# A DLRM interaction tower: embedding rows staged in DRAM by chunks, near and far loaded in one transfer each

## What is computed

```
x1 = relu(einsum('bhd,bmd,ohm->bod', e, e, W1) + b1)              # o = 128
x2 = relu(einsum('bhd,bmd,ohm->bod', x1[:, :64], e, W2) + b2)     # o = 128
z  = sum over d of concat(x1[:, 64:], x2)                         # 192 numbers per sample
```

## Time and profile before

| | |
|---|---|
| median of 3 runs | 2021.38 us (2020.23 to 2021.54) |
| profiled execution, its own time | 2020.18 us |
| its span in the profile | 2018.4 us |
| TensorE busy (matmul records) | 99% |
| VectorE, ScalarE, GpSimd busy | 95%, 83%, 68% |
| DMA engines, bytes over the span | 482.57 MB, 239 GB/s |

### The profile page before, as it was taken

One profiled execution on the slowest core, in us unless ns is written; L12 is line 12 of the kernel. 1 busy time (PEld: TensorE's weight loads), 2 busy tenths in 40 slices (PEclk: granted clock), 3 DMA queues, 4 the chain that ended last, 5 costly groups with the idle time before them and its releaser, 6 DMA issues.

```text
span 2018.4 us, 24272 instructions
## 1 busy us (share of the span) xinstructions
PE 1991.0 (99%) x7030; PEld 1322.2 (66%) x7030; DVE 1920.1 (95%) x672; ACT 1671.3 (83%) x4953; POOL 1370.3 (68%) x647
## 2 busy tenths in 40 slices
PE   5999999999999999999999999999999999999999
PEld 3666666666666666666666666666666666666664
DVE  6999999999999999999999999999999999999992
ACT  3888888888888888888888888888888888888884
POOL 5767867777677767768667668677767768677520
PEclk9999999999999999999999999999999999999999
DMA  7999999989989999999999999999999999998960
GB/s 214 261 262 245 263 239 243 259 240 243 258 240 243 254 244 243 252 247 242 250 250 241 249 252 240 248 251 241 249 251 239 247 253 240 247 254 240 244 174 11
DMA packets 272119, 482.57 MB, mean 239 GB/s; under 512 B 37473, under 2 KB 70753, under 8 KB 271858
## 3 DMA queue, kind: packets, MB, share of 16 engines
q1 hardware_dynamic: 244786, 404.58, 66.7%
q0 software_dynamic: 26624, 75.52, 21.7%
q10 hardware_dynamic: 576, 0.92, 0.1%
HBM read 313.10 MB, written 16.78 MB: 163 GB/s over the span
## 4 chain that ended last, share of the span: by engine, by line
PE 97%; DMA 1%; POOL 1%; issue 0%; SPq 0%; ACT 0%; DVE 0%; POOLq 0%; ACTq 0%
PE acc L618 21%; PE acc L630 19%; PE acc L637 19%; PE acc L631 19%; PE acc L642 16%; PE acc L621 1%; POOL gathered L272 0%; DMA plo_dma<-pnear 0%; PE x1p L721 0%; PE acc L721 0%; DMA gathered<-in_tables,idx_all 0%; DMA x1rep<-x 0%; DMA near<-emb_rows 0%; PE acc L728 0%; PE x1p L600 0%
## 5 line engine op out<-in xcount | busy, mean ns | idle before, releaser
L305 POOL TENSOR_TENSOR prod<-near,h 128x2048 f32<-128x2048 f32 x126 | 581.5, 4615 | 442.3 <-DMA near<-emb_rows 287.7
L630 PE MATMUL acc<-phi,w2lo 128*128 128x512 f32 x1664 | 704.4, 423 | 0.9 <-ACT phi L838 0.9
L631 PE MATMUL acc<-phi,w2hi 128*128 128x512 f32 x1664 | 651.8, 392 | 0.0
L534 DVE TENSOR_TENSOR pnear<-near,x1p 128x2048 f32<-128x2048 f32 x254 | 568.8, 2282 | 3.2 <-DMA plo_dma<-pnear 3.1
L527 DVE TENSOR_TENSOR pfar<-far,x1p 128x4096 f32<-128x4096 f32 x128 | 565.3, 4417 | 0.0
L272 POOL DMA_INDIRECT gathered<-in_tables,idx_all x256 | 495.5, 1935 | 71.5 <-issue 68.2
L845 ACT CAST phi<-pfar 128x2560 fp32r<-128x2560 f32 x128 | 300.2, 2345 | 216.5 <-PE acc L631 183.6
L618 PE MATMUL acc<-prod,w1T 128*128 128x512 f32 x1024 | 460.2, 592 | 1.5 <-DVE prod L507 1.5
L538 DVE TENSOR_TENSOR plo<-pnear,phi 128x3072 fp32r<-128x3072 f32 x128 | 433.5, 3386 | 0.0
L538 DVE TENSOR_TENSOR plo<-pfar,phi 128x2560 fp32r<-128x2560 f32 x128 | 361.7, 2826 | 41.1 <-ACT phi L845 40.7
L630 PEld LDWEIGHTS acc<-phi,w2lo 128*128 128x128 f32 x1664 | 313.1, 188 | 96.5 <-issue 30.4
(11 more groups left out here) (77 smaller groups left out, 1258.6 us busy)
## 6 DMA issues: line engine op xcount, KB each, us to landing
far<-emb_rows SPq DMA_DIRECT2D x512, 256.0 KB, 4.1
near<-emb_rows SPq DMA_DIRECT2D x510, 256.0 KB
plo_dma<-pnear POOLq DMA_DIRECT2D x128, 512.0 KB
x1rep<-x SPq DMA_DIRECT2D x255, 256.0 KB
h<-emb_rows SPq DMA_DIRECT2D x128, 256.0 KB
emb_rows<-gathered SPq DMA_DIRECT2D x127, 128.0 KB
rem_parts<-rem_hi SPq DMA_DIRECT2D x128, 64.0 KB
gathered<-in_tables,idx_all POOLq DMA_INDIRECT x256
```

The source lines that it names most:

```text
L305: nc.gpsimd.tensor_tensor(prod1[:, :, :], near[(u + 2) % 3][:, :, :], h0[odd][:, :].unsqueeze(1).to_broadcast([P, K1, N]), ALU.mult).then_ ...
L534: return nc.vector.tensor_tensor(pnear[:, a, :, :], near[u % 3][:, :, :], factor.unsqueeze(1).to_broadcast([P, K1, N]), ALU.mult)
L630: nc.tensor.matmul(acc2[s][:, :], w2lo[:, t, :], phi[:, t, :], start=(t == T_DMA), stop=False)
L631: mm = nc.tensor.matmul(acc2[s][:, :], w2hi[:, t, :], phi[:, t, :], start=False, stop=(t == T_SPLIT - 1))
```

## The change

- The DRAM array becomes one block of 64 rows x 512 numbers per chunk (128 KB, rows 2 KB apart).
- Tile k now pairs row i with row i + 4q + k. The four rows that a partition needs for `near` then lie side by side, and so do those for `far`: each becomes one transfer of 1 MB with 128 runs of 8 KB (it was four of 256 KB with runs of 2 KB). The weights are laid out to match (`diagonals`).
- The partitions of `gathered` are now (half of the pair, feature, part of the half). `store_copy` still writes 128 runs of 1 KB, in two blocks of 64 runs.
- The remainder works on 96 partitions in place of 64 (32 of them unused), `move_upper` moves 96, and six transfers place it in place of three.
- The table offsets are loaded by ScalarE in two halves (SP in one before), and the conversion of the indices is two copies in place of one.
- In the start, SP issues `h0` of chunk 0 and ScalarE all of `near` of chunk 0 (two tiles each before).

The diff, cut to its core; the other places follow from it (waits on the new counts, `c * N` in place of which stands `c`):

```diff
--- before.py
+++ after.py
@@ -20,10 +20,12 @@
-ROW = B * D + 1024
 SH = P // F
+CHUNK = 2 * F * N
 HALF = F // 2
 REM = 2 * HALF
+REM_ROWS = P - REM
@@ -58,7 +60,7 @@
-        emb = nc.dram_tensor("emb_rows", [2 * F, ROW], fp32, kind="Internal")
+        emb = nc.dram_tensor("emb_rows", [CHUNKS, CHUNK], fp32, kind="Internal")
@@ -82,10 +84,11 @@
-        rem_b = sb("rem_b", [HALF * GS, PAIR_GATHERS, D])
+        rem_b = sb("rem_b", [REM_ROWS, PAIR_GATHERS, D])
...
@@ -191,14 +194,15 @@
+        PLACES = 16 * 3 * 2
-        LOADS = 16 * (1 + K1)
+        LOADS = 16 * 2
...
-            return bass.AP(base.tensor, base.offset, [list(base.ap[0]), [SH, K1], [65, F], [1, SH]])
+            return bass.AP(base.tensor, base.offset, [list(base.ap[0]), [1, K1], [65, F], [SH, SH]])
@@ -236,20 +240,20 @@
         def store_copy(eng, f0, pair, s):
-            dst = bass.AP(emb, f0 * ROW + pair * (2 * N), [[ROW, F], [PAIR_GATHERS * D, GS], [1, PAIR_GATHERS * D]])
+            dst = bass.AP(emb, pair * (2 * CHUNK) + f0 * N, [[CHUNK, 2], [PAIR_GATHERS * D, P // 2], [1, PAIR_GATHERS * D]])
             eng.dma_start(dst, gathered[s][:, :, :]).then_inc(emb_stored, 16)
+        def load_h0(eng, c, s2, s3):
+            eng.dma_start(h0[s2][:, :], bass.AP(emb, c * CHUNK, [[N, F], [0, SH], [1, N]])).then_inc(near_in[s3], 16)
+
+        def load_near_tiles(eng, c, s3):
+            src = bass.AP(emb, c * CHUNK, [[N, F], [SH * N, SH], [1, K1 * N]])
+            eng.dma_start(near[s3][:, :, :].rearrange("p k n -> p (k n)"), src).then_inc(near_in[s3], 16)
...
-            sp.dma_start(table_row[:, :], a["table_rows"]).then_inc(ids_in, 16)
...
+            def load_far(c, s):
+                src = bass.AP(emb, c * CHUNK + HALF * N, [[N, F], [SH * N, SH], [1, K2 * N]])
+                sp.dma_start(far[s][:, :, :].rearrange("p k n -> p (k n)"), src).then_inc(far_in[s], 16)
             def move_upper(pair, s):
...
-                sp.dma_start(rem_b[:, :, :], gathered[s][HALF * GS:F * GS, :, :]).then_inc(rem_b_in, 16)
+                sp.dma_start(rem_b[:, :, :], gathered[s][REM:P, :, :]).then_inc(rem_b_in, 16)
...
                 for b, part in enumerate((rem_hi, rem_hi, rem_lo)):
-                    home = rem_parts[pair % 2][b * REM:(b + 1) * REM, :].rearrange("r (w n) -> r w n", w=2)
-                    sp.dma_start(home.bitcast(fp32), part[:, :].bitcast(fp32)).then_inc(rem_in, 16)
+                    for u in range(2):
+                        home = rem_parts[pair % 2][b * REM + u * HALF:b * REM + (u + 1) * HALF, :].rearrange("r (w n) -> r w n", w=2)
+                        sp.dma_start(home.bitcast(fp32), part[u * 2 * REM:u * 2 * REM + REM, :].bitcast(fp32)).then_inc(rem_in, 16)
@@ -376,8 +379,7 @@
             load_h0(sp, 0, 0, 0)
-            load_near_tiles(sp, 0, 0, range(0, K1 // 2))
-            load_near(sp, N, 1, 1)
+            load_near(sp, 1, 1, 1)
@@ -444,9 +446,12 @@
-            dve.wait_ge(ids_in, 32)
-            nc.vector.tensor_copy(ids_f[:, :, :].rearrange("r g (f q) -> r g f q", q=GS),
-                                  ids_n[:, :, :, :].rearrange("r q g f -> r g f q")).then_inc(ids_float, 1)
+            dve.wait_ge(ids_in, 48)
+            for w in range(2):
+                last = nc.vector.tensor_copy(
+                    ids_f[:, :, w * P // 2:(w + 1) * P // 2].rearrange("r g (f q) -> r g f q", f=F),
+                    ids_n[:, w * GS // 2:(w + 1) * GS // 2, :, :].rearrange("r q g f -> r g f q"))
+            last.then_inc(ids_float, 1)
@@ -768,9 +773,13 @@
+            for w in range(2):
+                nc.scalar.dma_start(table_row[w * P // 2:(w + 1) * P // 2, :],
+                                    a["table_rows"].rearrange("(f w q) one -> w f q one", w=2, q=GS // 2)[w]).then_inc(ids_in, 16)
             act.wait_ge(ident_ready, 1)
@@ -785,7 +794,7 @@
-            load_near_tiles(nc.scalar, 0, 0, range(K1 // 2, K1))
+            load_near_tiles(nc.scalar, 0, 0)
```

More of the change, by code:

```diff
@@ L82, in build_dlrm @@
         far = [sb(f"far_{s}", [P, K2, N]) for s in range(2)]
-        rem_b = sb("rem_b", [HALF * GS, PAIR_GATHERS, D])
-        rem_prod = sb("rem_prod", [HALF * GS, PAIR_GATHERS * D])
-        rem_hi = sb("rem_hi", [HALF * GS, PAIR_GATHERS * D], fp32r)
-        rem_lo = sb("rem_lo", [HALF * GS, PAIR_GATHERS * D], fp32r)
+        rem_b = sb("rem_b", [REM_ROWS, PAIR_GATHERS, D])
+        rem_prod = sb("rem_prod", [REM_ROWS, PAIR_GATHERS * D])
+        rem_hi = sb("rem_hi", [REM_ROWS, PAIR_GATHERS * D], fp32r)
+        rem_lo = sb("rem_lo", [REM_ROWS, PAIR_GATHERS * D], fp32r)
         rem_parts = [sb(f"rem_parts_{s}", [3 * REM, N], fp32r) for s in range(2)]
@@ L238, in store_copy, with load_near @@
         def store_copy(eng, f0, pair, s):
-            dst = bass.AP(emb, f0 * ROW + pair * (2 * N), [[ROW, F], [PAIR_GATHERS * D, GS], [1, PAIR_GATHERS * D]])
+            dst = bass.AP(emb, pair * (2 * CHUNK) + f0 * N, [[CHUNK, 2], [PAIR_GATHERS * D, P // 2], [1, PAIR_GATHERS * D]])
             eng.dma_start(dst, gathered[s][:, :, :]).then_inc(emb_stored, 16)
[L242 to L252, removed]
+        def load_h0(eng, c, s2, s3):
[3 more added lines that the diff above has]
+            eng.dma_start(near[s3][:, :, :].rearrange("p k n -> p (k n)"), src).then_inc(near_in[s3], 16)
+        def load_near(eng, c, s2, s3):
+            load_h0(eng, c, s2, s3)
+            load_near_tiles(eng, c, s3)
         def replicate_x1(eng, halves):
@@ L280, in remainder_products @@
                     pool.wait_ge(rem_lo_ready, pair)
-                nc.gpsimd.tensor_tensor(rem_prod[:, :], gathered[s][0:HALF * GS, :, :].rearrange("p g d -> p (g d)"),
+                nc.gpsimd.tensor_tensor(rem_prod[:, :], gathered[s][0:REM_ROWS, :, :].rearrange("p g d -> p (g d)"),
                                         rem_b[:, :, :].rearrange("p g d -> p (g d)"), ALU.mult).then_inc(rem_prod_ready, 1)
@@ L392, in _ @@
             sp.wait_ge(p1_ready, 1)
-            load_near(sp, 2 * N, 0, 2)
+            load_near(sp, 2, 0, 2)
             sp.wait_ge(w2_wide, 1)
             sp.wait_ge(w2_second, 1)
-            load_far(N, 1)
+            load_far(1, 1)
             def load_top():
@@ L428, in step @@
                         sp.wait_ge(emb_stored, STORES * (pair + 3))
-                    load_near(sp, (c + 3) * N, 1 - odd, u % 3)
+                    load_near(sp, c + 3, 1 - odd, u % 3)
                 if not odd and within(at, 5):
@@ L434, in step @@
                     sp.wait_ge(pfar_ready, c + 1)
-                    load_far((c + 2) * N, odd)
+                    load_far(c + 2, odd)
                 if at == 3:
@@ L473, in _ @@
             for u in range(2):
-                hi0, lo1, hi2 = (w1rem[u][:, b * REM + u:(b + 1) * REM:2] for b in range(3))
+                hi0, lo1, hi2 = (w1rem[u][:, b * REM + u * HALF:b * REM + (u + 1) * HALF] for b in range(3))
                 nc.vector.tensor_copy(hi0, w16hi[:, :].bitcast(fp32))
@@ L554, in step @@
                     dve.wait_ge(x1p_ready, 1)
-                dve.wait_ge(far_in[odd], 16 * K2 * (turn * (U // 2)) + 16 * K2 * (u // 2 + 1))
+                dve.wait_ge(far_in[odd], 16 * (turn * (U // 2)) + 16 * (u // 2 + 1))
                 if begun(at):
@@ L649, in _ @@
             tiles1(0, range(K1 // 2, K1))
-            pe.wait_ge(rem_in, 48)
+            pe.wait_ge(rem_in, PLACES)
             remainder1(0, 0)
@@ L676, in step @@
                     pe.wait_ge(p1_ready, c + 3)
-                    pe.wait_ge(rem_in, 48 * (pair + 2))
+                    pe.wait_ge(rem_in, PLACES * (pair + 2))
                     pe.wait_ge(z1_ready, c + 1)
@@ L770, in remainder_hi @@
                 if pair:
-                    act.wait_ge(rem_in, 48 * pair)
+                    act.wait_ge(rem_in, PLACES * pair)
                 nc.scalar.copy(rem_hi[:, :], rem_prod[:, :]).then_inc(rem_hi_ready, 1)
+            for w in range(2):
+                nc.scalar.dma_start(table_row[w * P // 2:(w + 1) * P // 2, :],
+                                    a["table_rows"].rearrange("(f w q) one -> w f q one", w=2, q=GS // 2)[w]).then_inc(ids_in, 16)
             act.wait_ge(ident_ready, 1)
```

## The result

The changed kernel takes 2124.45 us (median of 4 runs, 2118.89 to 2137.88) against 2020.81 us of before (4 runs). The ratio is 1.0524, 95% interval 1.049 to 1.0559: slower, +103.6 us. The profiled execution took 2121.54 us, its span is 2119.6.

The account below looks back on a forecast made before the run. TensorE bound the kernel before; DMA engines 0 and 1 would bind after, at 31.7 us a pair against 30.37. The profiled 2020.2 + 80 steady + 5 start = 2105, 2106 against the median; range 2019 to 2170 us.

Parts of the forecast that it names:

- The bound of before: In the steady part before the change, TensorE alone sets the time, 30.37 us per pair of chunks.
- Two engines for a store: The new store has outermost dimension 2, so two DMA engines carry it, 64 runs each.
- The store of pair 0: In the start, both stores put 128 runs on each of two engines; near of chunk 0 lands about 6 us later.
- A run of 1 KB: Price of one store or remainder packet on a DMA engine: 54 ns.
- Engines 0 and 1 become the bound: Stores add 6.0 us on these DMA engines; they need 31.7 us a pair against 30.37, so +80 us in all.
- The sign I had named for few engines: q1's mean share of the 16 DMA engines falls, with GB/s down, while time goes up.
- `near` and `far`: -1.2 us on every engine: Per pair, 128 runs of 2 KB (11.5 us) become 32 of 8 KB (10.3 us) on each DMA engine.
- Three issues more, +1.8 us of SP: Six transfers place the remainder in place of three, adding 1.8 us of SP's issue time per pair.
- bounds nothing: Six fewer SP issues per chunk save 7.2 us of SP a pair, said not to limit the time.
- The third rival: SP's in-order queue stalls behind store runs, delaying the replication of x1: 2170 us and up, chance 0.13.
- The start: Stores of pair 0 lie on the path before the steady part: +5 us, bounds 0 and +10.
- the offsets on ScalarE: Table offsets' loads in the start, counted among items within 0.5 us either way and left out.

Follow-up runs that it names:

- e1: The changed kernel with each store issued as two transfers of 64 partitions, one for each chunk of the pair: 2158.95 us.
- e2: The changed kernel with only the first of a pair's two stores issued as two transfers of 64 partitions: 2155.45 us.
- e3: The changed kernel with near and far each loaded by four transfers in runs of 2 KB, stores left on two engines: 2072.11 us.
- f1: e1 with near and far each loaded by four transfers of 256 KB in runs of 2 KB: 2097.07 us.
- f4: The kernel before with the remainder placed by six transfers of 32 partitions in place of three of 64: 2097.11 us.
- e4: e1 with the table offsets issued by SP ahead of the weights in place of ScalarE: 2159.34 us.
- h2: The changed kernel with the remainder's placement issued behind the near load in SP's step: 2547 us.
- h3: e3 with the remainder's placement issued behind the near load in SP's step: 2485 us.
- f2: e1 with near and far each loaded by two transfers of 64 partitions, runs still 8 KB: 2249.31 us.
- h1: f4 with the remainder's placement issued behind the near load in SP's step: 2475 us.

## Why the prediction came out near, and what in it was wrong

The forecast was 2106 us (2019 to 2170), slower at 0.76; measured were 2124.45. The number and the mean period (15.85 forecast, 15.87 measured) were close, and the mechanism behind them was wrong: that they met was luck. Even the period met only as a mean. A bound on every pair would have made every gap long, and 83 of 124 are those of before.

- **The bound of before** (TensorE alone, 30.37 us a pair) was right, and so was that faster loads give nothing.
- **Two engines for a store** was right: 130 packets in place of 144. So was the Trainium skill's rule by which the outermost dimension of 2 leads there ("DMA: Bandwidth & Descriptors", "Why a DMA increments its semaphore by 16 and not by 1"). The store of pair 0 held its readers 8.43 us where it was 2.56 (12.49 to 15.05): +5.9 us, forecast 6. A run of 1 KB cost 45 ns there, not 54. e1, with spread stores, has 5.6 us of the start back.
- **"Engines 0 and 1 become the bound"** is the step that failed. With the stores spread (e1, e2) the kernel is 31 to 35 us slower, not 100 faster, and e3 runs at 31.0 us a pair where its sum on these engines is 32.9. The sum of busy times against the period was not a bound: shares of a queue include the time a packet waits for its turn. The sign I had named for few engines, a lower q1 share (62.0% from 69.2%) in more time, came too, and means nothing. Whether the unspread stores are the better ones (35 us in e1, 25 from f1 to e3) for their two engines or for the two SP issues less is open; it wasn't tried.
- **"`near` and `far`: -1.2 us on every engine"** may hold as engine time (from 1100 to 1500 us q1's share fell from 69.2% for 83.13 MB to 62.0% for 79.22, less for each MB), but the longer runs acted on the time with the opposite sign, through the other queue: 62 us at 8 KB (e1 against f1), 52 with unspread stores (the change against e3), 30 at 4 KB. All of these kernels have six placements; what 8 KB runs would cost with three wasn't tried.
- **"Three issues more, +1.8 us of SP", costed at nothing**, is the largest miss: +76 us alone (f4). I had written that SP's time "bounds nothing", and looked at no path through its queue for these three. That SP is idle for part of a pair is true and no cover; each of the issues stands in a loop through GpSimd, SP and a transfer. The third rival had the right place (SP in order, ahead of the replication) with the wrong cause. Its stores do block SP (4.5 us in the median pair), and e1, without that, is no faster.
- **The start**: +11.5 us, forecast 5, bounds 0 and 10. The stores' part was sized about right: e1 has 5.6 us of it back. The other 5.9 stay in e1. Of them the offsets on ScalarE, left out, are some 1.2 us (e4) and six placements some 2.3 (f4 starts chunk 3 at 67.35 us, before at 65.08); the rest is open. In the change SP is held in one issue for 4.76 us (L358), behind the two stores and ahead of the placement, which is part of what e1 gives back.

The costs don't add up (76 and 62 against 104 in all), since they lengthen the same paths and the layout of the stores works against them. Some of the time is also the clock's: its mean grant in the profiled execution is 0.992 where it was 0.999, at most some 15 us of 2120 by an estimate from these two numbers. What is shown: three more placements cost 76 us by themselves, 8 KB runs cost 52 to 62 us beside six placements, and in f4 taking the gathers out of the loop gives the time back with all placements still there. That the changed kernel would be cured the same way wasn't tried; its chain also holds VectorE and the accumulating DMA.

## What to carry to other kernels

Idle time on each engine is not slack: follow one iteration around through every queue until it returns to the same instruction, and compare that loop with the period of the bound. A few more small transfers on an in-order queue can cost more than the bytes they move, and longer runs on one queue can slow another queue's transfer on the same engines. A forecast that meets the number proves nothing until the cause it named has been taken out once.

## What the runs showed of the hardware that I had not expected

- Beside packets of 4 KB from the accumulating DMA, SP's queue moved one 8 KB packet for each (108 to 98 in four microseconds), but some two of 2 KB (227 to 120). The accumulating DMA's transfer was 9.5 us (median) to landing beside 8 KB runs and 7.7 beside 2 KB (h2, h3); in the changed kernel it was 9.0, up to 12.8.
- Loads of 64 partitions gave 15.2 GB/s for each busy engine where 128 partitions gave 19.3 (f2, e1).
- SP was held by one small issue behind two stores on two engines each: 4.51 us in the median of 64, up to 8.70 (0.61 in e1, with the stores spread).
- TensorE, idle ahead of layer 1 for 312 us in 63 gaps (h1, in its wait list), fell to a mean granted clock of 0.915, and the kernel lost 455 us: a wait of 5 us in each pair cost some 7 (455 / 63).
